# Second attention of a four-layer graph network: the ring of gathered rows as eight slots of 512-byte rows, and the tensor engine's walk unrolled by eight

## The reference, cut to what matters

```
xl = x @ Wl + bl ;  xr = x @ Wr + br ;  e = edge_weight @ We
m = leaky_relu(xl[src] + xr[dst] + e, 0.2)        # one row of 128 for each edge
logits = m @ att
ex = exp(logits - segment_max(logits, dst)[dst])
out = segment_sum(xl[src] * ex, dst) / segment_sum(ex, dst) + bias_out
```

## Time and profile before

| | |
|---|---|
| median of three executions | 5094.93 us |
| the profiled execution: first to last instruction (span) | 5193.3 us |
| first attention, from its first L768 to its last | 97 to 970 us |
| second attention, from its first gather to the end of its last L803 | 1029.5 to 1807.7 us |
| PE, DVE, POOL, ACT busy over the span | 77%, 51%, 49%, 31% |
| gathers of the second attention (L756, narrow table) | 488, mean 946 ns |

### The profile page before, as it was taken

How to read it: one execution, slowest core, us unless ns; L and a number is a source line. 1 busy time by engine, 2 the same in 40 slices (tenths; PEclk the granted TensorE clock), 3 DMA queues, 4 the chain that set the end, 5 groups by cost and what they waited for, 6 DMA issues and landing times. The chain is left out here.

```text
span 5193.3 us, 93550 instructions
## 1 busy us (share of the span) xinstructions
PE 4017.0 (77%) x20700; PEld 3148.1 (61%) x20793; DVE 2652.4 (51%) x6184; ACT 1606.7 (31%) x3137; POOL 2568.2 (49%) x2650
## 2 busy tenths in 40 slices
PE   6999999777666656777667676667777699999997
PEld 4666666544444446666556666556666577777774
DVE  6777777755555532222322222322233677777775
ACT  3555655444444421111111111111111433333334
POOL 3555555356666555555355555355554244444440
PEclk7999999889999955555555555555555899999998
DMA  3333333222222221211111111111111233333330
GB/s 103 91 91 91 91 91 91 71 55 65 66 67 66 55 53 47 51 49 49 47 50 49 47 49 48 48 47 50 51 48 41 83 96 99 94 98 96 96 98 16
DMA packets 300265, 349.98 MB, mean 67 GB/s; under 512 B 105856, under 2 KB 232067, under 8 KB 299939
## 3 DMA queue, kind: packets, MB, share of 16 engines
q0 software_dynamic: 98528, 229.12, 16.4%
q1 hardware_dynamic: 182817, 92.67, 7.1%
q10 hardware_dynamic: 18850, 27.42, 1.9%
HBM read 332.87 MB, written 16.07 MB: 67 GB/s over the span
## 5 line engine op out<-in xcount | busy, mean ns | idle before, releaser
L988 POOL DMA_INDIRECT gath<-source_rows_narrow,idx x1176 | 1150.2, 978 | 993.8 <-SPq L973 461.9
L1016 PE MATMUL psum<-hot,pm 128*128 128x128 f32 x2928 | 758.3, 441 | 607.3 <-ACT pm L1071 585.3
L1016 PEld LDWEIGHTS psum<-hot,pm 128*128 128x128 f32 x2928 | 651.6, 327 | 697.5 <-ACT pm L1071 316.1
L1071 ACT ACTIVATE pm<-vs 128x512 f32<-128x512 f32 x366 | 231.1, 631 | 1880.6 <-DVE vs L1041 1476.2
L1006 PE MATMUL psum<-gine_lin,ea 32*128 32x128 f32 x2928 | 757.1, 436 | 29.6 <-DMA ea<-in_edge_attr 26.3
L1147 POOL DMA_INDIRECT gath<-source_rows,idx_all x416 | 429.3, 1032 | 633.9 <-DVE vs L1268 464.7
L1006 PEld LDWEIGHTS psum<-gine_lin,ea 32*128 32x128 f32 x2928 | 650.2, 323 | 115.3 <-issue 65.5
L756 POOL DMA_INDIRECT gath<-source_rows,idx_all x488 | 471.4, 966 | 441.7 <-PE psum L803 326.9
L756 POOL DMA_INDIRECT gath<-source_rows_narrow,idx_all x488 | 461.7, 946 | 335.8 <-remote 154.3
L1041 DVE TENSOR_TENSOR vs<-psum,gath 128x512 f32<-128x512 f32 x366 | 253.2, 692 | 669.7 <-issue 269.4
L1050 DVE TENSOR_TENSOR ACC<-ACC,psum 128x128 f32 x366 | 105.3, 288 | 808.4 <-remote 552.1
(11 more groups left out here) (238 smaller groups left out, 5685.1 us busy)
## 6 DMA issues: line engine op xcount, KB each, us to landing
rel<-rel_rows SPq DMA_DIRECT2D x244, 128.0 KB
ea<-in_edge_attr_tiles SPq DMA_DIRECT2D x416, 64.0 KB
ea<-in_edge_attr ACTq DMA_DIRECT2D x366, 64.0 KB
gath<-source_rows_narrow,idx POOLq DMA_INDIRECT x1176
gath<-source_rows,idx_all POOLq DMA_INDIRECT x904
rel<-quad_rel_rows SPq DMA_DIRECT2D x104, 128.0 KB
gath<-source_rows_narrow,idx_all POOLq DMA_INDIRECT x488
source_rows<-ACC SPq DMA_DIRECT2D x12, 512.0 KB, 2.9
```

The source lines that it names most:

```text
L988: pool.indirect_dma_start(out=gath[:, slot, j, 0:D], out_offset=None, in_=table1, in_offset=bass.IndirectOffsetOnAxis(ap=idx[:, slot, j:j ...
L1016: last = e.matmul(O[s], pm[:, s, j * P:(j + 1) * P], hot[:, s, j, :], start=(j == 0), stop=(j == SUBS - 1))
L1071: a.activation(pm[:, s, :], vs[:, s, :], ACT.Relu).then_inc(gi["msg"], 1)
```

## The change

The ring of the second attention gets eight slots. A view `ring` lays the same bytes of `gath` out as 8 slots of 4 x 128 floats, and `gat_edges` takes `gath` with 4 slots for two heads, `ring` with 8 for one. POOL waits for `o_ready` of the item eight before, so items 0 to 7 have nothing to wait for, and gathers go to contiguous rows. PE's walk in the second attention is written out in nine items and a loop body of eight that runs 14 times. The eight semaphores `gathered` are now shared by all layers, each of which counts on from where the one before left them; the third layer's four own ones go. ACT and DVE keep their walk of four.

```diff
+RING = 8
         gath = sb("gath", [P, 4, SUBS, 2 * D])
+        ring = gath[:, :, :, :].rearrange("p a j d -> p (a j d)").rearrange("p (r j d) -> p r j d", r=RING, j=SUBS)
-        def place(quad, m, layer):
-            return m % 2, layer * PAIRS + 2 * quad + m // 2, m, layer * -(-(ITEMS - m) // 4) + quad
+        def place(quad, m, layer, slots=4):
+            return m % 2, layer * PAIRS + slots // 2 * quad + m // 2, m, quad
-        def walk(e, front, back=nothing, mid=nothing, tail=nothing, layer=0):
+        def walk(e, front, back=nothing, mid=nothing, tail=nothing, layer=0, slots=4):
+            loops = (ITEMS - 2 - slots) // slots
+            assert loops * slots + slots + 2 == ITEMS
-            for i in range(5):
+            for i in range(slots + 1):
                 step(i, *(place_of(i - lag) for lag in range(min(i, 2) + 1)))
-            with e.Fori(0, (ITEMS - 6) // 4) as k:
-                for q in range(5, 9):
-                    step(4 * k + q, *(place(k + (q - lag) // 4, (q - lag) % 4, layer) for lag in range(3)))
+            with e.Fori(0, loops) as k:
+                for q in range(slots + 1, 2 * slots + 1):
+                    step(slots * k + q, *(place(k + (q - lag) // slots, (q - lag) % slots, layer, slots) for lag in range(3)))
-        gathered = [sem(f"gathered{s}") for s in range(4)]
+        gathered = [sem(f"gathered{s}") for s in range(RING)]
+        landings = [0] * RING
+        def landings_before(items, slots):
+            before = list(landings)
+            for slot in range(slots):
+                landings[slot] += 16 * SUBS * -(-(items - slot) // slots)
+            return before
...
+            slots = 4 * HEADS // heads
+            rows_of = gath if heads == HEADS else ring
+            landed_before = landings_before(ITEMS, slots)
...
                     for i in range(ITEMS):
-                        wait(pool, o_ready, before_h + heads * (i - 3))
+                        if i >= slots:
+                            pool.wait_ge(o_ready, before_h + heads * (i - slots + 1))
                         for j in range(SUBS):
                             pool.indirect_dma_start(
-                                out=gath[:, i % 4, j, 0:width], out_offset=None, in_=dram,
-                                in_offset=...).then_inc(gathered[i % 4], 16)
+                                out=rows_of[:, i % slots, j, :], out_offset=None, in_=dram,
+                                in_offset=...).then_inc(gathered[i % slots], 16)
...
-                        e.wait_ge(gathered[s4], 16 * SUBS * (turn4 + 1))
+                        e.wait_ge(gathered[slot], landed_before[slot] + 16 * SUBS * (round + 1))
...
-                    walk(e, front, back, mid, tail, number)
+                    walk(e, front, back, mid, tail, number, slots)
...
-                        sp.wait_ge(gi_gath[slot], 16 * SUBS * turn_of(slot, round))
+                        sp.wait_ge(gathered[slot], 16 * SUBS * turn_of(slot, round))
```

More of the change, by code:

```diff
@@ L220, in place_of @@
             def place_of(i):
-                return place(i // 4, i % 4, layer)
-            for i in range(5):
+                return place(i // slots, i % slots, layer, slots)
+            for i in range(slots + 1):
                 step(i, *(place_of(i - lag) for lag in range(min(i, 2) + 1)))
-            with e.Fori(0, (ITEMS - 6) // 4) as k:
-                for q in range(5, 9):
-                    step(4 * k + q, *(place(k + (q - lag) // 4, (q - lag) % 4, layer) for lag in range(3)))
+            with e.Fori(0, loops) as k:
+                for q in range(slots + 1, 2 * slots + 1):
+                    step(slots * k + q, *(place(k + (q - lag) // slots, (q - lag) % slots, layer, slots) for lag in range(3)))
             last = ITEMS - 1
@@ L753, in _, with front @@
                     for i in range(ITEMS):
-                        wait(pool, o_ready, before_h + heads * (i - 3))
+                        if i >= slots:
+                            pool.wait_ge(o_ready, before_h + heads * (i - slots + 1))
                         for j in range(SUBS):
                             pool.indirect_dma_start(
-                                out=gath[:, i % 4, j, 0:width], out_offset=None, in_=dram,
-                                in_offset=bass.IndirectOffsetOnAxis(ap=idx_all[:, i, j:j + 1], axis=0)).then_inc(gathered[i % 4], 16)
+                                out=rows_of[:, i % slots, j, :], out_offset=None, in_=dram,
+                                in_offset=bass.IndirectOffsetOnAxis(ap=idx_all[:, i, j:j + 1], axis=0)).then_inc(gathered[i % slots], 16)
                 @block.tensor
                 def _(e):
-                    def front(i, s, turn, s4, turn4):
-                        e.wait_ge(gathered[s4], 16 * SUBS * (turn4 + 1))
+                    def front(i, s, turn, slot, round):
+                        e.wait_ge(gathered[slot], landed_before[slot] + 16 * SUBS * (round + 1))
                         for h in range(heads):
@@ L767, in front @@
                             for j in range(SUBS):
-                                last = e.transpose(T[h][:, j * P:(j + 1) * P], gath[:, s4, j, h * D:(h + 1) * D], ident)
+                                last = e.transpose(T[h][:, j * P:(j + 1) * P], rows_of[:, slot, j, h * D:(h + 1) * D], ident)
                             last.then_inc(g_ready, 1)
@@ L796, in back, with tail @@
                             last.then_inc(pt_ready, 1)
-                    def tail(i, s, turn, s4, turn4):
+                    def tail(i, s, turn, slot, round):
                         wait(e, acc_done, before + i)
@@ L802, in tail @@
                             for j in range(SUBS):
-                                last = e.matmul(O[h], pt[:, h, j, :], gath[:, s4, j, h * D:(h + 1) * D],
+                                last = e.matmul(O[h], pt[:, h, j, :], rows_of[:, slot, j, h * D:(h + 1) * D],
                                                 start=(j == 0), stop=(j == SUBS - 1))
@@ L925, in build @@
         gi_ea = [sem(f"gine_ea_in{s}") for s in range(2)]
-        gi_gath = [sem(f"gine_gathered{s}") for s in range(4)]
         gi_landed, gi_free = sem("gine_landed"), sem("gine_free")
@@ L938, in gine_edges @@
             done = layer * ITEMS
+            landed_before = landings_before(GROUPS, 4)
             turns = layer * PAIRS
@@ L943, in turn_of @@
                 def turn_of(slot, round):
-                    return layer * -(-(GROUPS - slot) // 4) + round
+                    return landed_before[slot] // (16 * SUBS) + round
                 def by_group(e, body):
@@ L979, in landed @@
                     def landed(slot, round):
-                        pool.wait_ge(gi_gath[slot], 16 * SUBS * (turn_of(slot, round) + 1))
+                        pool.wait_ge(gathered[slot], 16 * SUBS * (turn_of(slot, round) + 1))
                         pool.nop().then_inc(gi_landed, 1)
@@ L985, in group @@
                             hold(pool, (gi_free, layer * (GROUPS - 4) + g - 3))
-                        hold(pool, (gi_idx[slot], 16 * (turn_of(slot, round) + 1)))
+                        hold(pool, (gi_idx[slot], 16 * (layer * -(-(GROUPS - slot) // 4) + round + 1)))
                         for j in range(SUBS):
@@ L1081, in mlp_edges @@
             ea_before, rel_before = 16 * GINE_LAYERS * PAIRS, 16 * 2 * PAIRS
-            gathered_before = [16 * SUBS * 2 * -(-(ITEMS - m) // 4) for m in range(4)]
+            gathered_before = landings_before(QUADS, 4)
             cleared, hot_t_done, hot_done, counted, h1_ready, h1_added, turned, h1_done, h2_ready, h2_added, h2_done, o_ready, acc_step = (
```

2 lines of the change are left out of this document (1 added, 1 removed).

## The result

Medians of 20 executions each: 5122.94 us for the changed kernel (5109.91 to 5140.61), 5117.07 us for the kernel before (5086.29 to 5132.23). The two medians lie only 5.9 us apart, the two means 11.7 us. The ratio that was estimated from all the runs together is 1.0025 with a 95% interval of 1.0013 to 1.0037, that is +12.8 us (+6.7 to +18.9), and the text goes by it. The changed kernel is slower by an amount that the interval tells from zero, but under the 0.3% that the prediction took as the least difference. The forecast was +15.5 us.

A forecast was written before the change was run, and what follows sets the result against it. The prediction took a closed loop of 6.10 us an item to bound the stage, PE's signals being held while POOL issues gathers back to back. Start +20.05 and end -4.6 gave +15.5 on 5094.93: 5110.4 us, range 5055 to 5136.

The forecast's parts named there:

- The likeliest case: Whole kernel: start term plus end term, 5110 us, own range 5103 to 5118; chance 0.50.
- PE's wait for the gather, value 0: Second attention, L768: removing this wait gains 0, since ACT's copy comes last; bounds 0 and 57.5 us.
- POOL's wait, an item unchanged: Second attention's loop: each arrival still gives leave for one item, so 6.10 us stays; value 0.
- Rival C: Second attention's loop: landing closes it, eight slots open it; item 5.01 us, 4972, with start term 4990; chance 0.16.
- The start, +20.05: Stage start: 16 more gathers delay PE's signal to ACT's L492; cost +20.05 us, bounds 0 and +21.4.
- the bound of 2.9: Stage start: PE's signals come 2.9 instead of 1.5 us behind the burst, making the start's upper bound +21.4.
- one idle time near 30 us: Sign at stage start: ACT's L492 idles once, near 30 us, ending 1 to 3 us behind the burst.
- rival B: Stage start: the hold is only part of the burst, 0 to half of 20.05 us; 5090 to 5101; chance 0.22.
- The end, -4.6: Stage end: four more items run with POOL silent, 4.95 instead of 6.10 us each; gain 4.6 us.
- the bound of 5: Stage end: upper bound of the gain from four more items with POOL silent, 5 us.
- The walk, layout and semaphores, 0: PE's unrolled walk, 512-byte rows and shared semaphores: value 0; bounds -3 and +3 (walk), -1 and +1 (rest).
- Rival D: Start of items: PE stays longer at its lower clock; +22 us on the likeliest case, 5132; chance 0.12.

The follow-up runs named there:

- two-gather kernels: Two of each item's four gathers in the second attention: on the kernel before, ratio 0.9745; on the changed kernel (items 2 and 3 keep four), 5060.49 us.
- the longer burst alone: Kernel before, ring of four, with 16 gathers that nobody reads issued behind the first 16 of the second attention: ratio 1.0049 (1.0037 to 1.0061).

## Why the prediction was right, step by step

The likeliest case came out: +15.5 us was forecast (to 5110.4), and +12.8 (+6.7 to +18.9) was measured. The two terms that the profile shows, +20.9 at the start and -5.3 at the end, add up to +15.6. That the median moved by 5.9 us alone says how near to the noise this is.

**PE's wait for the gather, value 0: right.** The 57.5 us of the old row came back as 57.3 us without a name, and L785 still starts some 0.1 us behind ACT's copy (1400.76 + 0.60 = 1401.36, L785 at 1401.50). A wait for two semaphores had been charged to the one that the change could remove, and the other stood right beside it.

**POOL's wait, an item unchanged: right.** 6.06 us at a depth of eight and of four on one chip; 5.96 us in the changed kernel's own profile, where two kernels of depth four on the fastest of the three chips have 5.98 and 5.99. (The first profile of before, whose span was 98 us above the median, has 6.04.) Rival C needed 5.01. The two-gather kernels agree: 4.95 at either depth.

**The start, +20.05: right in size and place, not in every step.** +20.9 in the changed kernel (48.4 - 27.5), +21.6 for the longer burst alone. ACT came 3.2 us behind the burst's end and not 1.5 (4.3 us in the kernel with the longer burst alone); the bound of 2.9 from the earlier trace rows was too small. The release came 1.6 us later than forecast, of which 0.7 came back, since three units were left for ACT then (1059.69, 1061.91, 1062.92) and not four; the first L785 came 0.9 us later than forecast. For the prediction had one idle time near 30 us, ended by the fourth unit's signal behind the burst. The runs have two, 7.63 and 22.71: the fourth unit's signal came late, but inside the burst, at 1035.86, and it was the fifth unit's that stayed out until the end. This is what rival B spoke of, and yet it won nothing, because the next unit was held as well. B's 0 to 10 us lie outside the interval of the longer burst alone.

The rule of the Trainium skill's page "SBUF — State Buffer" ("Who interferes with whom"), by which DMA and compute engines do not touch each other, would have given 5090. Of data it may hold: L820's eight products take 1.05 us at 1403.61 with gathers in flight, and as long at 1768.61 without. Of signals the runs show otherwise (ACT idle until 1059.69, where PE's last product had ended at 1039.30), and the prediction was right to take the rows.

**The end, -4.6: right.** 48.5 us in place of 53.8, -5.3, a little beyond the bound of 5. The unheld items took 4.95 us, as the earlier trace rows had said.

**The walk, layout and semaphores, 0: not contradicted.** The kernel with nothing but these has +0.11%, interval -0.02 to +0.24%.

**Rival D, a low clock for longer: not seen.** The granted clock rose from 0.50 to 1.00 some 17 us behind the first transposes on both sides (near 1074 us before, near 1082 us in the changed kernel), and items 0 to 8 took 49.4 us, as before (50.0).

**The range** was 81 us wide, because C could not be excluded from the profile of before. Its lower end, 5055, is a third of C's 123 us off 5094.93; it leaves out the start's 20 us, which C has too, and with them it would be near 5074. It was not asked how the 4.95 us of the earlier trace rows came about; that an item falls to it as soon as the burst is one gather shorter is what only the runs show. The pitch of 1.253 us has no row of its own: the earlier trace rows give 1.257 over the first sixteen gathers and 1.25 over the last eight of them, which changes the sum by 0.1 us.

**Open.** Why the signals are late. The runs narrow it: it depends on the gathers being close together and not on their bytes; and ACT, POOL and DVE all see it from PE. But the number in a row is not the whole condition. In the loop a signal 2.8 us into a row passes at once and one 3.7 us into it is held, while at the start of the stage ACT's L497 comes on time at 1027.11, 10 us into the burst. That DVE's signal reaches PE at 1405.87 while PE's own are out speaks against a stop for all engines alike; no run was made to test it. Whether the signals leave PE late or arrive late, no view tells: only the modelled end of a product and the start of its reader are seen.

## What to carry to other kernels

When two engines with unlike work both wait on "remote" and start together, look for a third engine's burst that ends just before, and add up the loop that they close; a deeper ring only helps if the wait that it removes is the last one of that loop. Count instructions in a row, not only their sum: here 16 gathers more ahead of a stage that had nothing to wait for cost their full issue time of 20 us, on another engine. Then look for what a burst is hidden behind: a first burst of 12 gathers cost no more than one of 8, beside PE's own 22.8 us of work ahead of the items. To learn what a burst costs, leave out one of its instructions and then two; the item fell by 1.1 us for the first and by nothing for the second.

## What the runs showed of the hardware

An indirect gather of 128 rows holds POOL for 0.94 to 0.95 us (the first behind a pause 1.03) with 0.30 us between two, for rows of 512 bytes and of 1 KB alike. Three gathers in a row (3.4 us), begun behind the weighted sum, leave PE's signals in time; four in a row make ACT and POOL start 1.1 to 1.4 us behind the fourth's end, for signals sent 3.7 us or more into the row, while those sent 1.2 and 2.8 us into it pass in 0.04 us. Of 32 in a row the last 20 us let no signal of PE through. A pause of 0.84 us between gathers did not let the signals pass, and with such pauses an item was longer by 0.8 us, the tensor engine's clock having a mean of 0.84.
